# V once a token, the projection of O at the start of the next body, and new orders on all engines

## What is computed

```python
qkv = x @ Wqkv                       # 128 -> 3 * 1024, 16 heads of 64; half of x's features shifted by a token
q, k = l2norm(q) * qs, l2norm(k) * ksc      # and rotated by tables with a scale
# windows of 32 queries, each sees its own 32 keys and the 32 before
sim = jnp.einsum('bhwie,bhwje->bhwij', bq, bk2) * QK_SCALE
attn = softmax(where(mask, -max, sim)); out = attn @ bv2
x = x + out @ Wo                     # 1024 -> 128
x = x + (a * gelu(gate)) @ W2 + b2   # a, gate = split(layernorm(shifted x) @ W1 + b1)
```

## Time and profile before

| | us |
|---|---|
| median of 3 runs | 2532.76 |
| profiled execution, its span | 2526.78, 2524.8 |
| TensorE busy, granted clock | 2108.4 (84%), 0.945 |
| VectorE, ScalarE, GpSimd busy | 1880.5 (74%), 1362.1 (54%), 1081.0 (43%) |
| from one body's `dg` to the next | 42.33 |

### The profile page before, as it was taken

The page is one execution under the profiler, slowest core; times in us unless marked ns, Lnnn a source line. Parts: engine busy times, 40 slices in busy tenths (PEclk is TensorE's granted clock), DMA queues, the critical chain, the costliest instruction groups (busy, mean ns, idle before and its releaser), DMA issues.

```text
span 2524.8 us, 85106 instructions
## 1 busy us (share of the span) xinstructions
PE 2108.4 (84%) x33737; PEld 1639.0 (65%) x33929; DVE 1880.5 (74%) x3469; ACT 1362.1 (54%) x2449; POOL 1081.0 (43%) x1385
## 2 busy tenths in 40 slices
PE   5988617889789898789898898987898987989894
PEld 3555405767677777667676777776676766767673
DVE  6898857777777777777777777777777776777764
ACT  3677614555465656455554556564565654555551
POOL 3000006454544545454555445454454545454530
PEclk7687959999999999999999999998999998999997
DMA  1000110000001000000000010000010000000000
GB/s 56 12 27 27 36 38 27 3 0 0 0 2 43 0 0 0 0 8 34 0 0 0 0 43 0 0 0 0 8 34 0 0 0 0 18 0 0 0 1 17
DMA packets 14798, 27.47 MB, mean 11 GB/s; under 512 B 4835, under 2 KB 10382, under 8 KB 13966
## 3 DMA queue, kind: packets, MB, share of 16 engines
q1 hardware_dynamic: 12670, 25.56, 2.9%
q10 hardware_dynamic: 2064, 1.05, 0.1%
HBM read 21.22 MB, written 5.37 MB: 11 GB/s over the span
## 4 chain that ended last, share of the span: by engine, by line
PE 50%; DVE 16%; issue 12%; ACT 5%; POOL 1%; DVEq 1%; DMA 0%; ACTq 0%; SPq 0%; POOLq 0%
PE scb L1214 8%; PE tb L1258 7%; PE wide L1234 6%; DVE nrm L1010 5%; PE wide L1203 4%; PE rawb L1176 4%; PE scb L1221 3%; PE rawb L1178 3%; PE rawb L1177 3%; PE tb L1288 3%; PE tb L1294 2%; PE tb L1289 2%; DVE dg L1057 2%; PE tb L1250 2%; ACT kT L858 2%
## 5 line engine op out<-in xcount | busy, mean ns | idle before, releaser
L810 POOL TENSOR_TENSOR part<-cs 128x256 f32<-128x256 f32 x384 | 279.0, 727 | 836.9 <-DVE cs L1006 834.6
L1006 DVE TENSOR_TENSOR cs<-rawb,rots 128x1024 f32<-128x1024 f32 x384 | 469.7, 1223 | 103.4 <-ACT sq L849 92.8
L849 ACT ACTIVATE sq<-rawb 128x512 f32<-128x512 f32 x384 | 229.2, 597 | 451.9 <-PE rawb L1178 446.9
L819 POOL TENSOR_TENSOR part<-part,nrm 128x512 f32<-128x512 f32 x384 | 397.2, 1066 | 156.3 <-DVE nrm L102 149.3
L865 ACT ACTIVATE V<-wide 128x512 f32<-128x512 f32 x384 | 230.1, 599 | 122.1 <-PE wide L1194 105.7
L1031 DVE TENSOR_REDUCE mx<-scb 128x8 f32<-128x512 f32 x192 | 132.3, 689 | 206.2 <-PE scb L1214 206.2
L811 POOL TENSOR_TENSOR part<-cs 128x256 f32<-128x256 f32 x384 | 280.1, 729 | 0.0
L1214 PE MATMUL scb<-kT,qT 64*32 64x64 f32 x12288 | 211.9, 218 | 65.1 <-ACT kT L858 33.0
L1234 PEld LDWEIGHTS wide<-V,pT 64*32 64x32 f32 x12288 | 185.3, 107 | 89.8 <-issue 89.8
L1234 PE MATMUL wide<-V,pT 64*32 64x65 f32 x12288 | 215.3, 219 | 24.6 <-issue 24.3
L1010 DVE TENSOR_REDUCE nrm<-sq 128x16 f32<-128x1024 f32 x192 | 232.1, 1209 | 0.0
(11 more groups left out here) (205 smaller groups left out, 4248.7 us busy)
## 6 DMA issues: line engine op xcount, KB each, us to landing
stage<-w_qkv_dram SPq DMA_DIRECT2D x6, 1536.0 KB, 6.7
scratch<-g_osb SPq DMA_DIRECT2D x8, 512.0 KB, 2.6
wo<-w_o_dram SPq DMA_DIRECT2D x6, 512.0 KB, 3.4
w<-w_dram SPq DMA_DIRECT2D x6, 384.0 KB, 3.0
w<-w_dram SPq DMA_DIRECT2D x6, 192.0 KB, 2.8
g_oc<-scratch SPq DMA_DIRECT2D x32, 32.0 KB
g_oden<-inverses SPq DMA_DIRECT2D x32, 32.0 KB
out_dram<-x ACTq DMA_DIRECT2D x1, 1024.0 KB, 5.1
```

The costliest lines, as they stand in the source:

```text
L810: nc.gpsimd.tensor_tensor(dst[:, :, 0, :], c[:, :, 0, :], s[:, :, 1, :], ALU.add)
L819: nc.gpsimd.tensor_tensor(p3, p3, nrm[:, 2, UH * u:UH * u + UH].unsqueeze(2).to_broadcast([P, UH, HD]), ALU.mult).then_inc(scaled, 1)
L849: nc.scalar.activation(sq[:, u % RING, :], rawb[:, u % 2, :], ACT.Square).then_inc(squared, 1)
L1006: nc.vector.tensor_tensor(dst, src, tab, ALU.mult).then_inc(turned, 1)
```

## The change

V is computed once a token: `V[:, 1]` and `V[:, 3]` are tokens 0 to 127 and 128 to 255, from 4 units of three products, which now go to the two banks of `scb` at the end of a body. `V[:, 0]` and `V[:, 2]`, the same tokens shifted by 32, are filled by three DMAs of SP a body (96, 32 and 96 partitions of 16 x 65 floats), for which weigh-values 0 waits (`v_moved`). The transposes of O use `wide`, and with the projection (in two halves) open the next body. GpSimd prepares x ahead of all eight scalings.

The order on TensorE: O 0 to 3, projection half 0, raw 0, projection half 1, spread, raw 1, q/k 0, 1, hidden 0, q/k 2, 3, hidden 1, raw 2, scores 0, q/k 4, 5, hidden 2, scores 1, raw 3, q/k 6, 7, means, probabilities 0, ffn-out, weigh 0, raw 4, scores 2, probabilities 1, weigh 1, scores 3, raw 5, probabilities 2, variances, weigh 2, raw 6, probabilities 3, weigh 3, raw 7, V 0 to 3.

On VectorE: `dg`, (at a layer's top: split 0, tables), rotation 0, xn, rotation 1, add attention, sum, (splits 1, 2), gates 0, 1, rotation 2, centring 0, gate 2, centring 1, rotation 3, sum, deviation, O 0, add FFN, rotation 4, centring 2, O 1, centring 3, rotation 5, sum, O 2, rotation 6, O 3, rotation 7, sum, roots.

```diff
-NV = 2 * NU
+NV = 2 * TT
...
+            def layer(l, more):
+                move_values(l * B)
+                if more:
+                    sp.wait_ge(w_low, sp.to_reg(WPARTS * (l + 1)))
+                    sp.dma_start(stage[:], w_qkv[l + 1]).then_inc(w_loaded, 16)
+                sp.wait_ge(y_ready, sp.to_reg(B * l))
+                sp.dma_start(wo[:], w_o[l]).then_inc(wo_in, 16)
+                move_values(l * B + 1)
+                sp.wait_ge(x_updated, sp.to_reg(B + l * B))
+                load_ffn(l)
+                with sp.Fori(2, B) as b:
+                    move_values(l * B + b)
+            def move_values(n):
+                sp.wait_ge(v_copied, sp.to_reg((n + 1) * NV))
+                for dst, src in ((V[WIN:P, 0, :, :], V[0:P - WIN, 1, :, :]), (V[0:WIN, 2, :, :], V[P - WIN:P, 1, :, :]),
+                                 (V[WIN:P, 2, :, :], V[0:P - WIN, 3, :, :])):
+                    sp.dma_start(dst, src).then_inc(v_moved, 16)
             sp.dma_start(wo[:], w_o[0]).then_inc(wo_in, 16)
             load_ffn(0)
-            with sp.Fori(1, DEPTH) as l:
-                sp.wait_ge(w_low, sp.to_reg(WPARTS * l))
-                sp.dma_start(stage[:], w_qkv[l]).then_inc(w_loaded, 16)
-                sp.wait_ge(y_ready, sp.to_reg(B * l))
-                sp.dma_start(wo[:], w_o[l]).then_inc(wo_in, 16)
-                sp.wait_ge(x_updated, sp.to_reg(B + l * B))
-                load_ffn(l)
+            sp.wait_ge(cleared, 1)
+            move_values(0)
+            sp.wait_ge(w_low, WPARTS)
+            sp.dma_start(stage[:], w_qkv[1]).then_inc(w_loaded, 16)
+            with sp.Fori(1, B) as b:
+                move_values(b)
+            with sp.Fori(1, DEPTH - 1) as l:
+                layer(l, True)
+            layer(DEPTH - 1, False)
...
-            nc.gpsimd.memset(V[:, :, :, HD:VW], 1.0)
+            nc.gpsimd.memset(V[0:WIN, 0, :, :], 0.0)
+            nc.gpsimd.memset(V[:, 1, :, HD:VW], 1.0)
+            nc.gpsimd.memset(V[:, 3, :, HD:VW], 1.0)
...
-                need_apart(pool, scaled, (n - 1) * NUN + NUN // 2)
+                need_apart(pool, added, n * NUN)
...
-                if u == NUN // 2 and F:
+                if u == 0 and F:
...
-                if A:
-                    for u in range(NUN // 2):
-                        apply_norms(n - 1, u, F)
                 if F:
                     prepare(n, b)
                 if A:
-                    for u in range(NUN // 2, NUN):
+                    for u in range(NUN):
...
-                half, u = j // NU, j % NU
-                nc.scalar.activation(V[:, u, 8 * half:8 * half + 8, 0:HD], wide[:, j % 2, :].rearrange("p (h d) -> p h d", d=HD),
+                half, i = j // TT, j % TT
+                nc.scalar.activation(V[:, 2 * i + 1, 8 * half:8 * half + 8, 0:HD], scb[:, j % 2, :].rearrange("p (h d) -> p h d", d=HD),
...
+                if C:
+                    copy_oT(t, 0)
+                    copy_oT(t, 1)
+                    copy_oT(t, 2)
+                    copy_oT(t, 3)
+                if F:
+                    square(n, 0)
+                    square(n, 1)
                 if A:
                     copy_qk(a, 0)
                     copy_qk(a, 1)
+                if E:
+                    gelu(r, 0)
                 if A:
                     copy_qk(a, 2)
                     copy_qk(a, 3)
                 if E:
                     gelu(r, 1)
                 if F:
                     square(n, 2)
                 if A:
+                    copy_qk(a, 4)
+                    copy_qk(a, 5)
+                    probs(a, 0)
                 if E:
                     gelu(r, 2)
                 if A:
+                    copy_qk(a, 6)
+                    copy_qk(a, 7)
                     probs(a, 1)
                 if F:
                     square(n, 3)
...
             def values(n, l, j):
-                half, u = j // NU, j % NU
+                half, i = j // TT, j % TT
                 if j == 0:
                     pe.wait_ge(w_low, WPARTS * l + 3)
-                if j < 2:
-                    need(pe, o_read, n * NG)
-                else:
+                if j >= 2:
                     pe.wait_ge(v_copied, n * NV + j - 1)
-                k0 = WIN * BLOCKS[2 * u]
-                x_hi, x_lo = xh[:, k0:k0 + P], xl[:, k0:k0 + P]
-                ps, cols = wide[:, j % 2, :], slice(2 * INNER + UW * half, 2 * INNER + UW * half + UW)
+                x_hi, x_lo = xh[:, WIN + P * i:WIN + P * i + P], xl[:, WIN + P * i:WIN + P * i + P]
+                ps, cols = scb[:, j % 2, :], slice(2 * INNER + UW * half, 2 * INNER + UW * half + UW)
                 mm(ps, x_hi, wh[:, cols], start=True, stop=False)
                 mm(ps, x_hi, wl[:, cols], start=False, stop=False)
                 mm(ps, x_lo, wh[:, cols], start=False, stop=True).then_inc(v_ready, 1)
-            def transpose_qk(a, u):
+            def transpose_qk(a, u, C):
                 pe.wait_ge(scaled, a * NUN + u + 1)
                 if u < 2:
-                    pe.wait_ge(v_copied, a * NV + NV - 1 + u)
+                    if C:
+                        pe.wait_ge(ot_copied, (a - 1) * NO + 3 + u)
                 else:
                     pe.wait_ge(tq_copied, a * NUN + u - 1)
                 for c in range(4):
             def scores(a, g):
                 if g in (0, 2):
                     pe.wait_ge(tq_copied, a * NUN + (NUN // 2 if g == 0 else NUN))
-                need(pe, pt_copied, a * NG + g - 1)
+                if g < 2:
+                    pe.wait_ge(v_copied, a * NV + 3 + g)
+                else:
+                    pe.wait_ge(pt_copied, a * NG + g - 1)
                 mm(scb[:, g % 2, :], idb[:], wmask[:], start=True, stop=False)
                 for at, u in enumerate(BLOCKS):
                     for h in range(GN):
             def weigh_values(a, g):
                 wait_apart(pe, cleared, pt_copied, a * NG + g + 1)
                 if g == 0:
-                    pe.wait_ge(v_copied, (a + 1) * NV)
                     pe.wait_ge(tq_copied, (a + 1) * NUN)
+                    wait_apart(pe, cleared, v_moved, 16 * VMOVES * (a + 1))
                 else:
                     pe.wait_ge(o_read, a * NG + g)
                 for h in range(GN):
                                   V[k0:k0 + KW, at // 2, GN * g + h, :], start=True, stop=True, tile_position=(k0, q0))
                 last.then_inc(o_ready, 1)
-            def transpose_o(t, k, E):
+            def transpose_o(t, k):
                 if k == 0:
                     pe.wait_ge(o_read, (t + 1) * NG)
-                    pe.wait_ge(root_ready, t + 2)
-                elif k == 1:
-                    need(pe, dev_ready, t)
-                    if E:
-                        pe.wait_ge(xn_ready, t)
-                else:
+                elif k >= 2:
                     pe.wait_ge(ot_copied, t * NO + k - 1)
-                i, c0 = k // 2, 4 * (k % 2)
+                i, c0 = k % 2, 4 * (k // 2)
                 for c in range(c0, c0 + 4):
-                    last = nc.tensor.transpose(tb[:, (k + 1) % 2, P * (c - c0):P * (c - c0) + P],
+                    last = nc.tensor.transpose(wide[:, k % 2, P * (c - c0):P * (c - c0) + P],
                                                O[:, i, 2 * c:2 * c + 2, :].rearrange("p h d -> p (h d)"), idf[:])
                 last.then_inc(ot_ready, 1)
-            def project_out(t):
-                pe.wait_ge(wo_in, 16 * layers_begun(t + 1))
-                pe.wait_ge(ot_copied, (t + 1) * NO)
-                for c in range(QC):
+            def project_out(t, half):
+                if half == 0:
+                    pe.wait_ge(wo_in, 16 * layers_begun(t + 1))
+                    need(pe, dev_ready, t)
+                pe.wait_ge(ot_copied, t * NO + 2 * half + 2)
+                for c in range(4 * half, 4 * half + 4):
                     last = mm(tb[:, 1, 0:T], wo[:, c, :], OT[:, c, :], start=c == 0, stop=c == QC - 1)
-                last.then_inc(y_ready, 1)
+                if half == 1:
+                    last.then_inc(y_ready, 1)
             def means(t, E):
+                pe.wait_ge(xf_ready, t + 1)
+                if E:
+                    pe.wait_ge(hid_ready, UP + (t - 1) * FC + 2)
+                mm(tb[:, 1, 0:T], mean1[:], xf[:], start=True, stop=True).then_inc(mean_ready, 1)
+            def variances(t, E):
                 if E:
                     pe.wait_ge(x_updated, B + t)
-                pe.wait_ge(xf_ready, t + 1)
-                mm(tb[:, 0, 0:T], mean1[:], xf[:], start=True, stop=True).then_inc(mean_ready, 1)
-            def variances(t):
                 pe.wait_ge(dsq_ready, t + 1)
                 for i in range(TT):
-                    last = mm(tb[:, 1, i:i + 1], dsq[:, P * i:P * i + P], mean1[:, 0:1], start=True, stop=True)
+                    last = mm(tb[:, 0, i:i + 1], dsq[:, P * i:P * i + P], mean1[:, 0:1], start=True, stop=True)
```

(47 more changed lines are left out.)

151 lines of the change are left out of this document (59 added, 92 removed).

## The result

| | before | after |
|---|---|---|
| median of 4 runs, us | 2533.69 | 2576.65 (2569.29 to 2579.12) |
| ratio, 95% interval | | 1.0163 (1.0140 to 1.0186) |
| profiled execution: span, us | 2524.8 | 2575.8 |
| layers alone (first raw product to the end of the span), us | 2149.2 | 2191.4 |
| ordinary body, mean of 36, us | 42.33 | 43.37 |

The change makes the kernel 43 us slower, where 75 us less were forecast, and the time lies far outside the range. The line "layers alone" is needed to compare profiles: behind the global attention, which no edit touches, the first raw product starts between 374 and 390 us in the thirteen traces of this study, so whole spans scatter by more than 10 us, and no run here shows why. Bodies and tops are measured from one root step on VectorE to the same step a body later; the 36 are the ordinary ones from body 7 to 47.

A forecast was written before the change was run, and what follows sets the result against it. PE is busiest, but DVE's last rotation, roots and `dg` set the body's end. Savings of 48 (40 bodies x 1.2), 18 (tops), 5 (first bodies) and 4 (tail), 75 us, gave 2452, plus 6.0 for the median: 2458 us, range 2405 to 2520.

The forecast's parts named there:

- The loop through all engines: Steady body of the changed kernel: a chain of seven pieces across the engines sets its length, 41.1 us in sum.
- (7): End of the body on PE: the four V units, 3.2 us.
- (1): Body's start: result and copy of the last V unit, first copy of transposed O, hand-overs, 1.55 us.
- (2): PE early in the body: two transposes, projection, raw 0, spread, raw 1, 6.4 us.
- (3): Square 1, then rotation 1 and add-attention on DVE, until hidden 1 may write its bank, 3.3 us.
- (4): PE: hidden 1, raw 2, scores 0, transposes of unit 4, 3.7 us.
- (5): ACT: copies, three table loads, Exps of groups 0 and 1, Gelu 2, square 3, copy of pT 0, hand-over, 8.4 us.
- (6): PE from weigh 0 to raw 7, with scores, transposes, squares and copies between, 14.5 us.
- rival B: Table loads on ACT wait for their activation's semaphore: body 42.7 us, kernel 2532 us, chance 0.09.
- rival D: On ACT, a switch costs more than its load's row when Exp and Gelu alternate: 2680 us, chance 0.03.
- E: V's moves inside SBUF land late for weigh 0; at 30 us, body 48.8, about 2800 us, chance 0.03.
- rival C: PE's stops lower its clock: 4 us of work a body at 1.2 GHz costs 3.4 more, 2621 us, chance 0.06.

The follow-up runs named there:

- experiment 4: Kernel before with V once a token alone (4 units, 4 copies, three moves on SP), all orders old: 2623.0 us, ratio 1.0337.
- experiment 1: Changed kernel with the third GELU issued ahead of the first Exp, so two table loads a body instead of four: 2429.25 us, ratio to before 0.957.
- experiments 3: Changed kernel with TensorE's second hidden matmuls waiting for VectorE's addition of the attention output, not the token copy behind it: 2519.74 us, ratio to before 0.9936.
- experiment 2: Changed kernel with four extra TensorE matmuls, result unused, in the stop ahead of the first weighing: 2533.62 us, ratio to before 0.9988.
- experiment 9: Changed kernel with two table loads a body, and VectorE's two token copies written as reductions: 2410.2 us, ratio to before 0.9517.
- experiment 6: Changed kernel with two table loads a body, and V computed twice (8 units, 8 copies, no moves): 2529.83 us, ratio to before 0.9998.
- Experiments 8: Changed kernel with two table loads a body, and the first weight split ahead of the diagonals at layer tops: 2420.67 us, ratio to before 0.955.
- kernel 10: Changed kernel with two loads, hidden matmuls behind the addition, copies as reductions, first weight split before the preceding body's roots: 2364.97 us, ratio to before 0.9354.

## Why the prediction was wrong

**What held.** What bounds the kernel was read rightly: VectorE holds the body's start, and V once alone gains nothing (experiment 4), though "gains nothing" left out that it loses. The loop through all engines is the path of the changed kernel: experiments 1 and 3 each took a wait out of it, and the body shrank. Its pieces, forecast and then measured in the body from 1506.74 to 1550.50: (7) 3.2, 3.11; (1) 1.55, 1.40; (2) 6.4, 6.72; (3) 3.3, 3.97; (4) 3.7, 3.72; (5) 8.4, 9.00; (6) 14.5, 15.84; sum 41.1, 43.76. The loads do start ahead of their Exp's semaphore: the one at 1531.47 ran while VectorE was still centring group 1, until 1532.32, so rival B is out. There are 186 of them, and the moves of V are in time: they land in 4.0 and 3.6 us, some 20 us before weigh 0, which waits for ACT. The page's rows for them:

```profile
V<-V SPq DMA_DIRECT2D x96, 390.0 KB, 4.0
V<-V SPq DMA_DIRECT2D x48, 130.0 KB, 3.6
```

Each of the activations shown stands 0.01 to 0.02 us behind its load, so rival D is out, and E too. The Trainium skill, "ScalarE: Activation LUTs", section "What ACT_TABLE_LOAD costs", has a drain of over a microsecond in the price of a switch; these rows disagree with it.

**How far off.** The forecast missed by 119 us. The ordinary bodies have about 91 of them: 43.37 instead of 41.1, of which 1.06 is the clock (experiment 2), 0.75 the loads beyond their 1.5 (experiment 2 against 1), and 0.46 what the loop is longer with two loads, 40.06 instead of 39.6 (experiment 9 takes 0.5 off by the copies alone). The tops have 25, the first bodies 5; the tail was 3 better.

**What failed, first: rival C was a mechanism of the forecast itself.** The prediction listed the clock as a rival with a chance of 0.06 and argued against it with PE's mean busy share (32.0 of 40 us at a clock of 1.00). The mean is the wrong reading. What the runs show is that one stop did it: behind 2.05 us the clock fell in 25 of 36 bodies; in the steady bodies of kernel 1, whose longest stop is the 1.08 us before the second hidden matmuls, it never fell; and with the 2.05 us filled it did not either. Why the same stop let it fall in 25 bodies and not in 11 stays open. The prediction had this very stop in its layout, as 1.9 us at weigh 0, counted it as one of eight, and gave the fall behind it a chance of 0.06. Its estimate of a fall, 4 us of work at the low level and 3.4 us lost, was too big for this place (1.5 us in a body that has it), so the kernel ended between C's 2621 and before. It has the slower sign of C and not its size; piece (6) is off by 1.34 through it. The row that should have been weighed is in the earlier trace rows: there a long stop was followed by the low level.

**Second: the loads were undersized.** The prediction let the two extra ones cost 1.5 us a body, because its layout without them came out at 39.6, held by other waits. Experiment 2 against 1 gives 2.25. The two loads and their hand-overs are 2.9, and three quarters of that lie on the path: with two loads the real loop is 40.06 and not 39.6 (39.56 without the copy beside POOL, experiment 9), and with four it is 42.31 and not 41.1. Piece (5) is off by 0.6. A load starts only when the activation ahead has ended, whereas two activations overlap by 0.1: the Exp is 0.65 to the start of the load behind it, not 0.52, and the pairs of copies ahead of a load 1.10 and 1.09, not 0.98. The steps of 0.52 and 0.49 hold where another activation follows (the second Exp, 0.54), and were used where a load does. That is 0.36; the rest is mostly the hand-over from the last copy to weigh 0, 0.30.

**Third: VectorE beside POOL.** The prediction named POOL's move as one that costs nothing, because the first scaled unit comes early enough. True, but POOL now prepares x beside the root steps, and scales beside add-attention. The root steps take 4.4 us instead of 3.3 (1509.95 to 1514.31), and the second half of the copy 1.04 instead of 0.29; piece (3) is 0.67 too long. Before, the copy stood where POOL was idle: the group of the second halves, 40 of them, of the kernel before, from the groups by line and shape (count, busy us, mean ns, idle before), then that of the kernel after and that of experiment 9's reductions.

```profile
L1048 DVE COPY xf<-X 64x256 f32 x40 | 11.7, 292 | 0.8 <-issue 0.2
```

```profile
L1067 DVE COPY xf<-X 64x256 f32 x40 | 41.6, 1040 | 0.6
```

```profile
L1067 DVE TENSOR_REDUCE xf<-X 64x256 f32 x40 | 16.7, 417 | 0.6
```

That experiments 3 and 9 each won time in the body's middle (1.0 and 0.5 us) shows it for the copy. For the root steps it is an argument: with V twice (experiment 6) they run before POOL is free to prepare, and the two-input ones take 0.23, where some take 0.43 to 0.66 in the changed kernel. No run moved POOL's preparation alone, and what these steps cost the path is not shown (PE's wait for `dg` is 0.19).

**Fourth: the tops.** Forecast 3.7 less, measured 1.3 more. `dg` first and the split second was wrong for PE, which needs the split for raw 0 and `dg` only after raw 0 and half a projection. The prediction had the splits "partly beside PE's transposes and projection"; they were, and still 6.4 us late. V once took away what hid them (experiment 6); that cast, subtraction and tables also run beside POOL is seen, and its share is not. Behind that stop the low clock again, 3.35 us for a half projection. Experiments 8 and 10 confirm the place: 3.4 and 8.6 us less, the second with the reductions and for 2.15 more in the body ahead.

**Ends.** First bodies: no gain (from the first raw product to the root step of body 2, 93.9 before and 93.8 after) against 5 forecast, and body 3 took 2.1 more. Tail 6.6 less, against 4.

**Two sums of the rivals** do not follow from the pieces, and neither bears on the result. Piece (5) holds three of the four loads, so doubling them adds 3.8 us and gives 44.9, not D's 46.0 (its 46.3 for a drain behind each load likewise). In B a top still gains 3.7 - 1.6 = 2.1, not 1.6, which gives 2529, not 2532.

## What to carry to other kernels

Before an order is accepted, list TensorE's stops one by one and price the long ones as if the clock fell behind them (here 2.05 us was long, and up to 1.6 was not); the mean busy share gave no warning here, and removing work from the busiest engine can slow it down. Count the table switches in every new order on ScalarE: each one that lies on a loop costs more than its 1.28 us once the stop that it makes on TensorE is counted (2.25 + 1.06 for two here). And when an engine's work is moved in time, look at what runs beside it on VectorE and GpSimd, not only at who waits for whom.

## What the runs showed of the hardware

- Behind one and the same stop of 2.05 us the clock fell in 25 of 36 bodies (43.8 among 42.3), and with the stop of 1.08 us gone from the body in 5 of 36 (43.0 among 41.4). Behind the stop of 4.66 us it fell in all 36, behind longest stops of 1.08 (experiment 1), 1.37 (the kernel before) and 1.4 to 1.6 us (experiment 6) in none.
- Four matmuls that nobody needs, in the stop of 2.05 us, bought 1.06 us a body; the time went from 2576.65 to 2533.62.
- A table load starts only after the activation ahead of it has ended (0.02 us behind it at the least, in all loads of the layers), and does not wait for the semaphore of its Exp (load from 1531.47, VectorE's centring until 1532.32), nor, at the tops of kernel 10, for that of a Gelu (load from 682.68, Gelu from 686.61).
- A copy of 64x256 between SBUF tensors takes 0.29 us with GpSimd idle, and 1.04 when a scaling of GpSimd has begun ahead of it; the reduction with the same values takes 0.41 and 0.42 beside the scalings.
- Behind the unchanged global attention the layers start anywhere from 374 to 390 us. Where that scatter comes from stays open.
